# Gated cross-attention and FFN layer: gate values, tanh and Wo^T handled before x(0)^T, u evicted by ScalarE, Z(7) evicted by VectorE

## The chip, the cores and the metric

The kernel runs on one core of a Trainium2 chip. The metric is the device time of one execution in microseconds (us); lower is better. The core has TensorE (PE in the profile, its weight loads PEld), VectorE (DVE), ScalarE (ACT), GpSimd (POOL), and SyncE (SP), which only issues DMA transfers here. Each engine executes its own list of instructions in order; semaphores order the lists against each other.

## The reference

There are 16 batch rows, each of 128 queries and 128 context positions, with 256 features, in float32.

```
LN(x) = (x - mean) / sqrt(var + 1e-5)            over the 256 features
Q = LN(x) @ Wq.T + bq        K = ctx @ Wk.T + bk
attn = softmax(where(mask, -inf, Q @ K.T))
x1 = x + tanh(g_xattn) * ((attn @ ctx) @ Wo.T + bo)
y  = clip(LN(x1) @ sign(W).T * scale + bias, -100, 100)
out = x1 + tanh(g_ffn) * y
```

## The kernel before, in words

All instruction lists are written out by hand; there is no scheduler. The 16 rows are handled as 8 groups of two, numbered 0 to 7; L is 7. The projections of Q and K are folded: the product of Wk and the centred Wq is formed once (wqk), a bias vector u comes with it, and the scores are xn^T times K, where K = wqk applied to ctx^T, plus u. For Z = ctx times Wo^T, Wo^T carries the factor tanh(g_xattn), so the attention output is P times Z directly. Operands of the large products are split in a high and a low fp32r part: ScalarE evicts the high part from PSUM, VectorE subtracts it to get the low part.

For one group TensorE does, in this order: K projection (12 matmuls), transposes of the normalised x of the next group, P times Z of the previous group, scores, transposes of ctx of the next group, transposes of x1 of the previous group, Z projection (12), transposes of the softmax numerators p, and the FFN product of the previous group (8). VectorE computes the residual x1, the masked scores and their minimum (t_sb), the statistics of x1, the low parts x1T_lo and cT_lo, the clip, the FFN scaling (y_scaled), the sum out_sb, and the statistics of x three groups on. GpSimd computes the reciprocal standard deviations (a pow), x + bo (xb_sb, `add_bo`), the mask terms and y_biased. ScalarE evicts K, xT, Z, p^T and the high parts, computes the exponentials and normalises x for groups 2 and up.

The prologue matters for the change. SP issues its transfers in the order Wq, Wk, x(0), ctx(0), Wo, mask, the two gates (4 bytes each), x(1), ctx(1), x(2), bo and so on. TensorE transposes ctx(0), computes u into a few columns of the PSUM bank ps_O, transposes Wo into the bank of Z (L629), waits for the normalised x(0) and transposes it (`transpose_x(0)`), computes the first half of K(0) (L679), broadcasts the two gates over the partitions by a matmul with a row of ones (L818, into other columns of the bank of u; it waits for `u_ready` and for the gates), computes the second half of K(0), transposes ctx(1), and does the scores of group 0 (L721). VectorE evicts u (L557), then xT(0) (L559), then computes the statistics of x(1) (`stats_x(1)`, L427 and L430), then woT_lo (L562). ScalarE evicts the first half of K(0) (L243), computes tanh of both gates (L245), evicts woT_hi with the factor tanh (L248), then the second half of K(0) (L250). GpSimd does the mask terms of group 0, `norm_of_x(1)` (four small operations, L300 to L306), `normalise_x(1)` (L314), `norm_of_x(2)`, then bo times tanh (bo_g, L390), then `add_bo(0)` (L369).

In the tail, TensorE computes the Z of the first row of group 7, the scores of group 7 and the Z of its second row, transposes p (`transpose_p(L)`, L729), does the FFN product of group 6 row by row (`ffn_before_last`), then `attend_last` (L769). VectorE does `mask_and_min(L)` (L455) and then `split_x1T(L - 1)` (L447); `ffn_before_last` waits for the latter. ScalarE does the two exponentials, evicts Z(7) (L219) and then p^T (L230).

Of the kernel before, what the change touches and what calls it, by code (L numbers as in the profile page):

```python
# [6 lines left out]
ACT = mybir.ActivationFunctionType  # L7
# [12 lines left out]
def gated_xattn_ffn(nc, x, ctx, mask, g_xattn, g_ffn, wq, bq, wk, bk, wo, bo, w_ffn, scale_ffn, bias_ffn, out):  # L20
# [12 lines left out]
    G = B // GB  # L33
    T = GB * P
    L = G - 1
# [5 lines left out]
    with ExitStack() as stack:  # L41
# [3 lines left out]
        def sem(name):  # L45
            return stack.enter_context(nc.semaphore(name))

        def bank(name):
# [90 lines left out]
        x1T_hi_done, x1T_lo_done, scaled_done, biased_done, clip_done, out_done, pool_clip_done, pool_out_done = (  # L139
            sem(n) for n in ("x1T_hi_done", "x1T_lo_done", "scaled_done", "biased_done", "clip_done", "out_done",  # L140
                             "pool_clip_done", "pool_out_done"))
        last_biased_done = sem("last_biased_done")

        rows = lambda g: slice(g * GB, (g + 1) * GB)
# [2 lines left out]
        @block.sync  # L147
        def _(sp):
            def load_x(g):
                sp.dma_start(x_sb[:, rows(g), :], x_rows[:, rows(g), :]).then_inc(x_loaded[g], 16)  # L150

            def load_ctx(g):
                sp.dma_start(ctx_sb[:, rows(g), :], ctx_rows[:, rows(g), :]).then_inc(ctx_loaded[g], 16)

            sp.dma_start(wq_sb[:], wq.rearrange("(c p) d -> p c d", p=P)).then_inc(wq_loaded, 16)
            sp.dma_start(wk_sb[:], wk.rearrange("(c p) d -> p c d", p=P)).then_inc(wk_loaded, 16)
            load_x(0)
            load_ctx(0)
            sp.dma_start(wo_sb[:], wo.rearrange("(c p) d -> p c d", p=P)).then_inc(wo_loaded, 16)
            sp.dma_start(mask_u8[:], mask.rearrange("(o b) k -> o b k", o=1).to_broadcast([P, B, P])  # L160
                         ).then_inc(mask_loaded, 16)
            for k, v in enumerate((g_xattn, g_ffn)):
                sp.dma_start(gate_row[:, k:k + 1], v.rearrange("(o d) -> o d", o=1)).then_inc(gates_loaded, 16)
            load_x(1)
            load_ctx(1)
            load_x(2)
            sp.dma_start(bo_sb[:], bo.rearrange("(o d) -> o d", o=1).to_broadcast([P, D])).then_inc(bo_loaded, 16)
            sp.dma_start(w_sb[:], w_ffn.rearrange("(c p) d -> p c d", p=P)).then_inc(w_loaded, 16)
            load_ctx(2)
            load_x(3)  # L170
            sp.dma_start(scale_sb[:], scale_ffn.rearrange("(o d) -> o d", o=1).to_broadcast([P, D])
                         ).then_inc(scale_loaded, 16)
            sp.dma_start(bias_sb[:, 0, :], bias_ffn.rearrange("(o d) -> o d", o=1).to_broadcast([P, D])
                         ).then_inc(bias_loaded, 16)
            load_ctx(3)
            for g in range(4, G):
                load_x(g)
                load_ctx(g)
            for g in range(L):
                if g == L - 2:  # L180
                    sp.wait_ge(pool_out_done, GB)
                else:
                    sp.wait_ge(out_done, g + 1)
                sp.dma_start(out_rows[:, rows(g), :], out_sb[:, rows(g), :]).then_inc(stored, 16)
            for b in range(GB):
                sp.wait_ge(out_done, L + b + 1)
                sp.dma_start(out_rows[:, L * GB + b, :], out_sb[:, L * GB + b, :]).then_inc(stored, 16)
            sp.wait_ge(stored, 16 * (G + 1))

        @block.scalar  # L190
        def _(act):
# [25 lines left out]
            def evict_Z(g):  # L217
                act.wait_ge(Z_prod, g + 1)
                nc.scalar.copy(Z_sb[:, g % 2], ps_Z).then_inc(Z_done, 1)  # L219
# [18 lines left out]
            act.wait_ge(ps_wqk_ready, DC)  # L238
            nc.scalar.copy(wqk_hi[:, 1], ps_wqk[1]).then_inc(wqk_hi_ready, 1)
            evict_cT_hi(0)  # L240
            act.wait_ge(u_ready, 1)
            act.wait_ge(ps_K0_ready, 1)
            nc.scalar.activation(K_sb[:, 0, 0], ps_K0[0], ACT.Identity, bias=u_col[:, 0:1]).then_inc(K_done, 1)  # L243
            act.wait_ge(ps_gates_ready, 1)
            nc.scalar.activation(tanh_g[:], ps_gates, ACT.Tanh).then_inc(tanh_ready, 1)  # L245
            act.wait_ge(ps_woT_ready, 1)
            act.wait_ge(tanh_ready, 1)
            nc.scalar.activation(woT_hi[:], by_chunk(z_bank), ACT.Identity, scale=tanh_g[:, 0:1]).then_inc(woT_hi_ready, 1)  # L248
            act.wait_ge(ps_K0_ready, DC)
            nc.scalar.activation(K_sb[:, 0, 1], ps_K0[1], ACT.Identity, bias=u_col[:, 1:2]).then_inc(K_done, 1)  # L250
            evict_cT_hi(1)
# [26 lines left out]
            evict_x1T_hi(L - 1)  # L278
            exp(L, 0)
            exp(L, 1)  # L280
            evict_Z(L)
            evict_PT(L)

            for b in range(GB):
# [4 lines left out]
        def _(pool):  # L289
# [94 lines left out]
            mask_terms(0)  # L384
            norm_of_x(1)
            normalise_x(1)
            norm_of_x(2)
            pool.wait_ge(tanh_ready, 1)
            pool.wait_ge(bo_loaded, 16)
            nc.gpsimd.tensor_scalar(bo_g[:], bo_sb[:], tanh_g[:, 0:1], 1.0, ALU.mult, ALU.mult).then_inc(bo_g_ready, 1)  # L390
            pool.wait_ge(bo_g_ready, 1)
            add_bo(0)
            mask_terms(1)
# [29 lines left out]
        def _(dve):  # L423
            def stats_x(g):
                dve.wait_ge(x_loaded[g], 16)
                for b in range(GB):
                    nc.vector.bn_stats(bn_x[:, g * GB + b], x_sb[:, g * GB + b]).then_inc(bn_x_done, 1)  # L427
                for b in range(GB):
                    dve.wait_ge(bn_x_done, GB * g + b + 1)
                    nc.vector.bn_aggr(mv_x[:, g * GB + b], bn_x[:, g * GB + b]).then_inc(mv_x_done, 1)  # L430
# [122 lines left out]
            nc.vector.tensor_tensor(wqk_lo[:, 1], ps_wqk[1], wqk_hi[:, 1].bitcast(F32), ALU.subtract  # L553
                                    ).then_inc(wqk_lo_ready, 1)
            split_cT(0)
            dve.wait_ge(ps_u_ready, 1)
            nc.vector.tensor_copy(u_col[:], ps_u).then_inc(u_ready, 1)  # L557
            dve.wait_ge(xT_prod, 1)
            nc.vector.tensor_scalar(xT[:, 0], ps_xT, 1.0, None, ALU.add).then_inc(xT_done, 1)  # L559
            stats_x(1)  # L560
            dve.wait_ge(woT_hi_ready, 1)
            nc.vector.scalar_tensor_tensor(out=woT_lo[:], in0=by_chunk(z_bank), scalar=tanh_g[:, 0:1],  # L562
                                           in1=woT_hi[:].bitcast(F32), op0=ALU.mult, op1=ALU.subtract
# [24 lines left out]
            residual(L - 1)  # L588
            stats_x1(L - 1)
            add_x1(L - 3)  # L590
            mask_and_min(L)
            split_x1T(L - 1)
            for b in range(GB):
                r = L * GB + b
                dve.wait_ge(p_done, r + 1)
# [29 lines left out]
        def _(pe):  # L625
# [136 lines left out]
                accumulate(F_before_last[b], pairs).then_inc(F_prod, 1)  # L762

            def attend_last(b):
                pe.wait_ge(Z_done, G)
                pe.wait_ge(PT_done, GB * L + b + 1)
                if b == 0:
                    pe.wait_ge(x1_done, GB * L)
                nc.tensor.matmul(last_O[b], PT_sb[:, L % 2, b], Z_sb[:, L % 2, b], start=True, stop=True  # L769
                                 ).then_inc(O_prod, 1)  # L770
# [39 lines left out]
            last.then_inc(ps_u_ready, 1)  # L810
            pe.wait_ge(wo_loaded, 16)
            transposes(by_chunk(z_bank), wo_sb).then_inc(ps_woT_ready, 1)
            transpose_x(0)
            project_first_K(0)
            pe.wait_ge(gates_loaded, 32)
            pe.wait_ge(ones_ready, 1)
            pe.wait_ge(u_ready, 1)
            nc.tensor.matmul(ps_gates, ones_row[:], gate_row[:], start=True, stop=True).then_inc(ps_gates_ready, 1)  # L818
            project_first_K(1)
            transpose_ctx(1)  # L820
            first_scores()
# [27 lines left out]
            Z_of(L, 0)  # L849
            scores(L)  # L850
            Z_of(L, 1).then_inc(Z_prod, 1)
            transpose_p(L)
            ffn_before_last(0)
            ffn_before_last(1)
            attend_last(0)
            attend_last(1)
# [31 lines left out]
```

## Time and profile before

| | |
|---|---|
| median of 3 runs | 75.99 us (75.79 to 76.14) |
| profiled execution, its own time | 76.03 us |
| its span in the trace | 74.2 us |
| busy, share of the span: PE / DVE / POOL / ACT | 92% / 78% / 72% / 57% |
| granted TensorE clock | 0.994 of full speed |

All times inside the trace are counted from the start of the span; the execution's own time is 1.8 us longer than the span. Rows of the timeline give the start, the duration, the engine, the line of the kernel, the operation, and the tiles written and read. In brackets stands how long the engine was idle before the row, and which instruction ended the wait.

### The profile page before, as it was taken

The page shows a single profiled execution, that of the slowest core. Times are in us where ns is not written, and L with a number is a line of the kernel's source. Part 1 is how long each engine was busy: PE and PEld are TensorE (multiplying, and loading weights), DVE is VectorE, ACT ScalarE, POOL GpSimd, SP SyncE. Part 2 cuts the span into 40 slices and gives each one's busy share as a digit, 9 for nine tenths or more (in the row PEclk, how much of TensorE's full clock was granted, in tenths as well). Part 3 has the DMA queues.
Part 4 walks back from the last instruction along what each step waited for, and adds up shares of the span by engine and source line. Part 5 has one row for each costly group of instructions (what it writes and reads, how often), then busy time and mean ns, then how long its engine had stood idle before and what let it go on. Part 6 is the DMA issues. An engine that isn't in the chain of part 4 may idle for free.

```text
span 74.2 us, 1595 instructions
## 1 busy us (share of the span) xinstructions
PE 68.2 (92%) x509; PEld 64.1 (86%) x509; DVE 57.8 (78%) x187; ACT 42.4 (57%) x116; POOL 53.7 (72%) x107
## 2 busy tenths in 40 slices
PE   4999999999999999998999999999999999998800
PEld 4988789998999999997999999999999999884500
DVE  0085697894947688699899989998959899759980
ACT  1502519599799639771996397749575906534000
POOL 4000605889899999896989898989899859959700
PEclk9999999999999999999999999999999999999997
DMA  0989999999940000004000400030012000412043
GB/s 4 274 202 335 299 263 309 288 366 357 344 145 5 4 0 9 9 0 141 0 0 0 141 0 9 18 124 0 0 67 75 0 9 0 146 54 87 9 165 109
DMA packets 8229, 8.10 MB, mean 109 GB/s; under 512 B 537, under 2 KB 8093, under 8 KB 8221
## 3 DMA queue, kind: packets, MB, share of 16 engines
q1 hardware_dynamic: 8212, 8.00, 34.7%
q8 instruction: 4, 0.07, 0.4%
q14 instruction: 5, 0.03, 0.2%
q10 hardware_dynamic: 8, 0.00, 0.0%
HBM read 5.90 MB, written 2.10 MB: 108 GB/s over the span
## 4 chain that ended last, share of the span: by engine, by line
PE 45%; POOL 24%; DVE 13%; DMA 6%; issue 4%; ACT 1%; SPq 1%; POOLq 1%; DVEq 0%
PE ps_Z L634 9%; PE ps_K L634 8%; DMA x_sb<-in_x_dram 6%; PE ps_xT L629 6%; PE ps_F L634 6%; POOL xb_sb L369 6%; PE ps_O L737 5%; PE ps_S L634 4%; POOL y_biased L373 4%; POOL rstd_x L302 3%; DVE bn_x L427 3%; PE ps_cT L629 2%; POOL rstd L321 2%; PE ps_S L729 2%; POOL y_clip L346 1%
## 5 line engine op out<-in xcount | busy, mean ns | idle before, releaser
L373 POOL TENSOR_TENSOR y_biased<-y_scaled,bias_g 128x256 f32<-128x256 f32 x14 | 11.7, 857 | 2.1 <-DVE y_scaled L512 1.0
L369 POOL TENSOR_TENSOR xb_sb<-x_sb,bo_g 128x256 f32<-128x256 f32 x16 | 11.4, 736 | 0.1
L224 ACT ACTIVATE p_sb<-t_sb,smin 128x128 f32<-128x128 f32 x16 | 6.4, 401 | 8.1 <-DVE smin L455 8.0
L634 PE MATMUL ps_Z<-woT_hi,cT_hi 128*128 128x256 f32 x32 | 9.8, 305 | 0.0
L214 ACT ACTIVATE K_sb<-ps_K,u_col 128x256 f32<-128x256 f32 x14 | 5.8, 469 | 6.6 <-PE ps_K L634 6.6
L634 PE MATMUL ps_Z<-woT_hi,cT_lo 128*128 128x256 f32 x32 | 9.0, 282 | 0.0
L634 PE MATMUL ps_Z<-woT_lo,cT_hi 128*128 128x256 f32 x32 | 9.0, 282 | 0.0
L466 DVE SCALAR_TENSOR_TENSOR x_sb<-ps_O,recip_p,xb_sb 128x256 f32<-128x256 f32 x14 | 6.1, 479 | 2.9 <-PE ps_O L737 1.8
L634 PE MATMUL ps_K<-cT_hi,wqk_hi 128*128 128x256 f32 x28 | 8.2, 293 | 0.0
L634 PE MATMUL ps_K<-cT_lo,wqk_hi 128*128 128x256 f32 x28 | 7.9, 283 | 0.0
L634 PE MATMUL ps_K<-cT_hi,wqk_lo 128*128 128x256 f32 x28 | 7.9, 283 | 0.0
L634 PEld LDWEIGHTS ps_S<-K_sb,xT 128*128 128x128 f32 x56 | 7.2, 191 | 0.5 <-issue 0.2
L634 PE MATMUL ps_S<-K_sb,xT 128*128 128x128 f32 x56 | 7.5, 277 | 0.0
L737 PE MATMUL ps_O<-Z_sb,PT_sb 128*128 128x256 f32 x28 | 7.2, 379 | 0.0
L634 PE MATMUL ps_F<-wT,x1T_hi 128*128 128x256 f32 x26 | 7.1, 306 | 0.0
L427 DVE BATCH_NORM_STATS2 bn_x<-x_sb 128x6 f32<-128x256 f32 x16 | 5.9, 412 | 1.0 <-DMA x_sb<-in_x_dram 1.0
L442 DVE TENSOR_TENSOR cT_lo<-ps_cT,cT_hi 128x512 fp32r<-128x512 f32 x8 | 5.5, 685 | 1.5 <-ACT cT_hi L197 1.5
L204 ACT ACTIVATE xn<-x_sb,nmr_x,rstd_x 128x256 f32<-128x256 f32 x12 | 6.6, 602 | 0.1
L634 PE MATMUL ps_F<-wT,x1T_lo 128*128 128x256 f32 x26 | 6.5, 282 | 0.0
L512 DVE SCALAR_TENSOR_TENSOR y_scaled<-ps_F,rstd,scale_g 128x256 f32<-128x256 f32 x12 | 5.3, 479 | 1.4 <-POOL rstd L321 1.1
L634 PEld LDWEIGHTS ps_Z<-woT_lo,cT_hi 128*128 128x128 f32 x32 | 6.1, 191 | 0.0
L634 PEld LDWEIGHTS ps_Z<-woT_hi,cT_hi 128*128 128x128 f32 x32 | 6.1, 190 | 0.0
(138 smaller groups left out, 201.9 us busy)
## 6 DMA issues: line engine op xcount, KB each, us to landing
x_sb<-in_x_dram SPq DMA_DIRECT2D x8, 256.0 KB, 7.3
ctx_sb<-in_ctx_dram SPq DMA_DIRECT2D x8, 256.0 KB, 7.2
out_dram<-out_sb SPq DMA_DIRECT2D x7, 256.0 KB, 2.1
wq_sb<-in_L_xattn_Wq_dram SPq DMA_DIRECT2D x1, 256.0 KB, 2.9
wk_sb<-in_L_xattn_Wk_dram SPq DMA_DIRECT2D x1, 256.0 KB, 3.1
wo_sb<-in_L_xattn_Wo_dram SPq DMA_DIRECT2D x1, 256.0 KB, 5.0
mask_u<-in_mask_BxS_bk_dram SPq DMA_DIRECT2D x1, 256.0 KB, 5.4
w_sb<-in_L_ffn_weights_dram SPq DMA_DIRECT2D x1, 256.0 KB, 6.9
```

Of the source, the lines that this page charges most:

```text
L204: nc.scalar.activation(xn[:, r], x_sb[:, r], ACT.Identity, scale=rstd_x[:, r:r + 1], bias=nmr_x[:, r:r + 1]).then_inc(xn_done, 1)
L214: nc.scalar.activation(K_sb[:, g % 2, m], ps_K[:, m], ACT.Identity, bias=u_col[:, m:m + 1]).then_inc(K_done, 1)
L224: nc.scalar.activation(p_sb[:, g % 2, b], t_sb[:, g % 2, b], ACT.Exp, scale=-1.0, bias=smin[:, r:r + 1], accum_out=psum_p[:, r:r + 1]).the ...
L369: nc.gpsimd.tensor_tensor(xb_sb[:, r], x_sb[:, r], bo_g[:], ALU.add).then_inc(xb_done, 1)
L373: nc.gpsimd.tensor_tensor(y_biased[:, g % 2, b], y_scaled[:, g % 2, b], bias_g[:, 0], ALU.add).then_inc(biased_done, 1)
L427: nc.vector.bn_stats(bn_x[:, g * GB + b], x_sb[:, g * GB + b]).then_inc(bn_x_done, 1)
L442: nc.vector.tensor_tensor(cT_lo[:, g % 2], ps_cT, cT_hi[:, g % 2].bitcast(F32), ALU.subtract).then_inc(cT_lo_done, 1)
L466: nc.vector.scalar_tensor_tensor(out=x1_sb[:, r], in0=ps_O[:, b], scalar=recip_p[:, r:r + 1], in1=xb_sb[:, r], op0=ALU.mult, op1=ALU.add). ...
L512: nc.vector.scalar_tensor_tensor(out=y_scaled[:, g % 2, b], in0=ps_F[:, b], scalar=rstd_1[:, r:r + 1], in1=scale_g[:], op0=ALU.mult, op1=A ...
L629: last = nc.tensor.transpose(dst[:, c, b * P:(b + 1) * P], src[:, b, c * P:(c + 1) * P], ident[:])
L634: last = nc.tensor.matmul(dst, lhsT, rhs, start=(n == 0), stop=(n == len(pairs) - 1))
L737: last = nc.tensor.matmul(ps_O[:, b], PT_sb[:, g % 2, b], Z_sb[:, g % 2, b], start=True, stop=True)
```

## The change

SP issues the two gate transfers ahead of the mask. TensorE does the matmul of the gates right after the transposes of Wo, ahead of x(0)^T. The eviction of u goes from VectorE to ScalarE; ScalarE then does tanh and woT_hi ahead of the first half of K(0). VectorE does the statistics of x(1) ahead of the copy of x(0)^T. GpSimd computes bo_g ahead of `norm_of_x(2)`. In the tail VectorE splits x1T(6) before it handles the scores of group 7, and evicts Z(7) after them; TensorE does the first FFN product of group 6 before it transposes p of group 7.

```diff
@@ SP
+            for k, v in enumerate((g_xattn, g_ffn)):
+                sp.dma_start(gate_row[:, k:k + 1], v.rearrange("(o d) -> o d", o=1)).then_inc(gates_loaded, 16)
             sp.dma_start(mask_u8[:], mask.rearrange("(o b) k -> o b k", o=1).to_broadcast([P, B, P])
                          ).then_inc(mask_loaded, 16)
-            for k, v in enumerate((g_xattn, g_ffn)):
-                sp.dma_start(gate_row[:, k:k + 1], v.rearrange("(o d) -> o d", o=1)).then_inc(gates_loaded, 16)
@@ ScalarE
             evict_cT_hi(0)
-            act.wait_ge(u_ready, 1)
-            act.wait_ge(ps_K0_ready, 1)
-            nc.scalar.activation(K_sb[:, 0, 0], ps_K0[0], ACT.Identity, bias=u_col[:, 0:1]).then_inc(K_done, 1)
+            act.wait_ge(ps_u_ready, 1)
+            nc.scalar.copy(u_col[:], ps_u).then_inc(u_ready, 1)
             act.wait_ge(ps_gates_ready, 1)
             nc.scalar.activation(tanh_g[:], ps_gates, ACT.Tanh).then_inc(tanh_ready, 1)
             act.wait_ge(ps_woT_ready, 1)
             act.wait_ge(tanh_ready, 1)
             nc.scalar.activation(woT_hi[:], by_chunk(z_bank), ACT.Identity, scale=tanh_g[:, 0:1]).then_inc(woT_hi_ready, 1)
+            act.wait_ge(u_ready, 1)
+            act.wait_ge(ps_K0_ready, 1)
+            nc.scalar.activation(K_sb[:, 0, 0], ps_K0[0], ACT.Identity, bias=u_col[:, 0:1]).then_inc(K_done, 1)
...
             exp(L, 0)
             exp(L, 1)
-            evict_Z(L)
             evict_PT(L)
@@ GpSimd
             normalise_x(1)
-            norm_of_x(2)
             pool.wait_ge(tanh_ready, 1)
             pool.wait_ge(bo_loaded, 16)
             nc.gpsimd.tensor_scalar(bo_g[:], bo_sb[:], tanh_g[:, 0:1], 1.0, ALU.mult, ALU.mult).then_inc(bo_g_ready, 1)
+            norm_of_x(2)
             pool.wait_ge(bo_g_ready, 1)
@@ VectorE
             split_cT(0)
-            dve.wait_ge(ps_u_ready, 1)
-            nc.vector.tensor_copy(u_col[:], ps_u).then_inc(u_ready, 1)
+            stats_x(1)
             dve.wait_ge(xT_prod, 1)
             nc.vector.tensor_scalar(xT[:, 0], ps_xT, 1.0, None, ALU.add).then_inc(xT_done, 1)
-            stats_x(1)
...
             add_x1(L - 3)
+            split_x1T(L - 1)
             mask_and_min(L)
-            split_x1T(L - 1)
+            dve.wait_ge(Z_prod, G)
+            nc.vector.tensor_copy(Z_sb[:, L % 2], ps_Z).then_inc(last_Z_done, 1)
@@ TensorE
             def attend_last(b):
-                pe.wait_ge(Z_done, G)
+                pe.wait_ge(last_Z_done, 1)
...
             transposes(by_chunk(z_bank), wo_sb).then_inc(ps_woT_ready, 1)
-            transpose_x(0)
-            project_first_K(0)
+
             pe.wait_ge(gates_loaded, 32)
             pe.wait_ge(ones_ready, 1)
             pe.wait_ge(u_ready, 1)
             nc.tensor.matmul(ps_gates, ones_row[:], gate_row[:], start=True, stop=True).then_inc(ps_gates_ready, 1)
+            transpose_x(0)
+            project_first_K(0)
             project_first_K(1)
...
+            ffn_before_last(0)
             transpose_p(L)
-            ffn_before_last(0)
             ffn_before_last(1)
```

## Rows read from the trace of the kernel before

**Rows 1.** Stretches: length; busy us (instructions) of PE, PEld, DVE, ACT, POOL; clock, DMA.
```profile
21.00:34.82 13.82, 13.51 (x110) 13.06 (x108) 10.81 (x33) 9.41 (x26) 12.30 (x24) 1.00 0.09 31
34.82:63.45 28.63, 28.63 (x232) 28.16 (x233) 25.85 (x80) 19.34 (x54) 25.71 (x47) 1.00 0.09 29
```

**Rows 2.** Timeline, TensorE: the gates, K(0), ctx(1) and the first scores.
```profile
9.37 0.42 PEld L629 LDWEIGHTS ps_xT<-ident,xn 128*128 128x128 f32 x4 [0.47 <-DVE xn L550]
...
10.72 0.38 PE L818 MATMUL ps_O<-gate_row,ones_row 1*128 1x2 f32 x2
11.03 0.50 PE L679 MATMUL ps_F<-cT_hi,wqk_hi 128*128 128x256 f32 x2
11.85 0.60 PE L629 MATMUL ps_cT<-ident,ctx_sb 128*128 128x128 f32 x4
...
12.18 0.97 PEld L721 LDWEIGHTS ps_S<-K_sb,xT 128*128 128x128 f32 x8
```

**Rows 3.** Timeline, VectorE at the same place.
```profile
10.16 0.14 DVE L557 COPY u_col<-ps_O 128x2 f32<-128x2 f32 x1
10.23 0.68 DVE L559 TENSOR_SCALAR xT<-ps_xT 128x512 f32<-128x512 f32 x1
10.82 0.74 DVE L427 BATCH_NORM_STATS2 bn_x<-x_sb 128x6 f32<-128x256 f32 x2
11.48 0.30 DVE L430 BATCH_NORM_AGGREGATE mv_x<-bn_x 128x2 f32<-128x6 f32 x2
```

**Rows 4.** DMA issues: size, us to landing; the second from 4.3 to 4.8 us, x(1).
```profile
mask_u<-in_mask_BxS_bk_dram SPq DMA_DIRECT2D x1, 256.0 KB, 5.4
x_sb<-in_x_dram SPq DMA_DIRECT2D x1, 256.0 KB, 5.2
...
3.24 0.47 SPq L160 DMA_DIRECT2D mask_u<-in_mask_BxS_bk_dram  x1
```

**Rows 5.** Timeline, groups 1 and 2: the normalised x and GpSimd.
```profile
13.56 1.10 POOL L314 TENSOR_SCALAR xn<-x_sb,rstd_x,nmr_x 128x256 f32<-128x256 f32 x2
...
15.06 0.71 POOL L302 TENSOR_TENSOR rstd_x<-ve_x,minus_half 128x2 f32<-128x2 f32 x1
...
16.30 0.48 POOL L390 TENSOR_SCALAR bo_g<-bo_sb,tanh_g 128x256 f32<-128x256 f32 x1
...
16.35 1.09 ACT L204 ACTIVATE xn<-x_sb,nmr_x,rstd_x 128x256 f32<-128x256 f32 x2
...
17.68 0.60 PE L629 MATMUL ps_xT<-ident,xn 128*128 128x128 f32 x4
```

**Rows 6.** Waits of TensorE (total, times, longest), then timeline, where it waits and later.
```profile
PEld ps_xT L629 <- DVE x_sb L466: 0.5, 1, 0.5
...
29.95 0.54 DVE L519 TENSOR_SCALAR y_clip<-y_biased,lim 128x512 f32<-128x512 f32 x1
30.06 0.99 POOL L321 TENSOR_TENSOR rstd<-ve,minus_half 128x2 f32<-128x2 f32 x1
31.09 0.88 DVE L512 SCALAR_TENSOR_TENSOR y_scaled<-ps_F,rstd,scale_g 128x256 f32<-128x256 f32 x2 [0.60 <-POOL rstd L321]
...
41.01 0.88 DVE L466 SCALAR_TENSOR_TENSOR x_sb<-ps_O,recip_p,xb_sb 128x256 f32<-128x256 f32 x2
...
41.94 0.43 PEld L629 LDWEIGHTS ps_xT<-ident,x_sb 128*128 128x128 f32 x4
```

**Rows 7.** Timeline of the tail.
```profile
64.16 0.69 DVE L447 TENSOR_TENSOR x1T_lo<-ps_xT,x1T_hi 128x512 fp32r<-128x512 f32 x1
...
64.85 0.14 PEld L729 LDWEIGHTS ps_S<-ident,p_sb 128*128 128x128 f32 x1 [0.25 <-ACT p_sb L224]
...
65.78 0.48 DVE L601 SCALAR_TENSOR_TENSOR y_scaled<-ps_F,rstd,scale_g 128x256 f32<-128x256 f32 x1 [0.78 <-PE ps_F L634]
...
66.34 1.41 POOL L373 TENSOR_TENSOR y_biased<-y_scaled,bias_g 128x256 f32<-128x256 f32 x2 [0.79 <-DVE y_scaled L601]
...
68.93 1.18 POOL L326 TENSOR_TENSOR rstd<-ve,minus_half 128x1 f32<-128x1 f32 x2
```

More of the change, by code:

```diff
@@ L141, in gated_xattn_ffn @@
                              "pool_clip_done", "pool_out_done"))
+        last_Z_done = sem("last_Z_done")
         last_biased_done = sem("last_biased_done")
```

## The prediction

> **What bounds the kernel now.** I read the busy time by stretch first. From 34.82 to 63.45 us TensorE is busy in all 28.63 us, at full clock; from 21.00 to 34.82 it lacks 0.31 us [rows 1]. So the body is TensorE's own work, and a gain must take instructions off TensorE's list or remove one of its few waits. The list of waits names one in the body: the weight load for x1^T waits 0.5 us for VectorE's residual [rows 6]. The timeline then tells why: VectorE had stood idle for 0.60 us before y_scaled at 31.09, until GpSimd's pow had ended [rows 6], and the chain of waits runs back on GpSimd from there, nearly without a gap, to 14.75 us. GpSimd's list from 14.7 to 31 us thus sets TensorE's only stall in the body. The same row of residuals one group later (41.01, 0.88 long, ends 41.89) stands just ahead of the weight load that uses it (41.94) [rows 6]: after the stall VectorE and TensorE run side by side with no reserve, so what TensorE gains at 34.8 is what VectorE gains there, and it is kept to the tail. In the tail the chain is FFN product of group 6, y_scaled (65.78, after 0.78 idle), y_biased on GpSimd (66.34), clip, the last pow (68.93) [rows 7], and then VectorE's last operations and the store.
>
> **The change, part by part.**
>
> *Gates ahead of x(0)^T.* The matmul of the gates starts at 10.72 and the second half of K(0) at 11.03, so it takes 0.31 us of TensorE's path [rows 2]. Its new place is a gap: PEld is idle for 0.47 us before 9.37, that is from 8.90 on, waiting for the normalised x(0) [rows 2]. Before its wait it has to see u evicted: the u matmuls end at about 8.65, and a copy of 128x2 takes 0.14 on VectorE [rows 3]; on ScalarE the row is not there for this shape, and I take 0.2 (tanh of the same shape is the nearest; bounds 0.14 and the 0.3 that would put it at 8.95). The matmul can then start at 8.95 and is through by 9.27, 0.1 ahead of need. If the cover is gone, it costs what it overlaps, at most 0.31, and the gain of this step is nothing. Then also the gates must have landed. No row gives their landing. They now take the mask's place in the list, issued at 3.24 and some 0.4 later; the mask issued there landed 5.4 later, at 8.64 [rows 4]. I take that as the bound from above for the first and 8.7 for the second, still ahead of 8.95. From below it is somewhere after their issue, which costs nothing. The mask itself is issued 0.6 later and lands at about 9.3; its term on GpSimd (0.4 us) falls in an idle stretch that lasts until the statistics of x(1), so nothing is late.
>
> The Trainium skill (DMA: Bandwidth & Descriptors, Queues, rings and completion order) says that completion is not FIFO per issuing engine, and that a one-engine copy can complete while earlier 16-engine ones are still open. Its table of the fixed cost gives about 2.0 us; an estimate by it has the gates in by 5.7 to 8.7 us, on the same side as the bound above. No row shows their landing.
>
> *K(0), xT(0), statistics.* The second half of K(0) now follows the first directly and takes 0.82 us as before (11.03 to 11.85) [rows 2]. The weight load for the scores, at 12.18 before, could be at 11.8. What may be late instead is xT(0), now behind the statistics: VectorE drops the u copy and starts the statistics at 10.16 instead of 10.82 (0.66 earlier), and the copy of xT ends where the statistics ended, 11.78 [rows 3], less 0.07 for the u copy: 11.7. That is just in time. x(1) landed at about 9.6 (issued near 4.4, 5.2 to landing) [rows 4], 0.5 before it is needed. ScalarE has tanh and woT_hi (0.7 us) behind it at about 10.4, before the first half of K(0) is ready at 10.8, and evicts both halves without being late. So the scores move by 0.3 to 0.4.
>
> *Normalised x(1), bo_g, normalised x(2).* Statistics 0.66 earlier put GpSimd's xn(1) at 12.90 instead of 13.56, ending 14.00 [rows 5]; TensorE wants it at about 14.4. Then bo_g (0.48) runs to 14.5, in what would else be a wait for the statistics of x(2). bo landed at about 12.5. The pow of x(2) moves from 15.06 by 0.2 only, and ScalarE's xn(2), 16.35 to 17.44, moves to 17.24 at the end. Its transposes stood at 17.68 [rows 5] and can be at 17.34 at the earliest. This caps TensorE's gain in the prologue at about 0.3. I take 0.3 (bounds 0, if the gates' cover fails, and 0.4). But `add_bo(0)`, the next on GpSimd, gains both: 0.2, and 0.48 because bo_g no longer stands before it: 0.67.
>
> *The stall at 34.8.* GpSimd's list runs from there to the pow at 30.06 without waiting, as far as I can follow its inputs: y_scaled of group 0 is ready at about 24.1 and wanted at 24.6, the statistics of x(4) at 24.9 and wanted at 26.0, those of x1(1) at 28.1 and wanted at 29.1. So the pow ends 0.67 earlier and y_scaled starts at 30.42 instead of 31.09. VectorE is free for it at 30.2 (the clip ends at 30.49 [rows 6], less 0.3). So the residual that TensorE waits for is 0.67 earlier. TensorE without the stall would be earlier by 0.3 of the prologue plus 0.31 (its idle) to 0.5 (that of the weight load), 0.6 to 0.8. The smaller of both is 0.62 to 0.67; I take 0.65 for prologue and stall together. Bounds: 0.3 if nothing of the stall goes, 0.8 if all of it does.
>
> The pow took 0.99 there and 0.71 for the same shape at 15.06 [rows 5, 6], while VectorE's clip ran beside it. The Trainium skill (SBUF — State Buffer, Who interferes with whom) has a cause: VectorE and GpSimd share a port pair, and an operation in a two-port mode blocks the other for its whole length. By that rule a pow that starts 0.67 earlier and a clip that starts 0.3 earlier still overlap, by about 0.2 instead of 0.4, and the residual could gain up to 0.2 more than I take. In other places the same rule can make new collisions, the subject of the last rival.
>
> *Tail.* VectorE's split of x1T(6) (0.69, the next operation starts 0.61 after it) goes ahead of the scores. Its input is there at 63.14, so it ends at 63.8 and the first t_sb starts 0.19 later than before (63.78 instead of 63.59). The second one waited for its scores and is late by 0.06 only. Both exponentials are late by 0.19, and the transpose of the second p, which PEld did at 64.85 after 0.25 idle [rows 7], could be at 65.05. TensorE fills this with the first FFN product (4 matmuls, 0.49), which starts at 64.47 and ends at 64.96; the two transposes then find p ready at once. The second FFN product ends 0.25 to 0.3 earlier. Z(7) is evicted by VectorE at 64.65 (its last matmul ends at 64.60); the price is that of the xT copy of the same shape, 0.68 [rows 3], so to 65.33, with `attend_last` wanting it at 65.6. It falls in VectorE's 0.78 idle before y_scaled [rows 7]; behind it stand the two reciprocals (0.23) and y_scaled, which starts at 65.5 instead of 65.78. So y_biased, the clips and the last pow start 0.27 earlier; the variance that the pow also needs moves with the residuals, 0.27. I take 0.27. Bounds: minus 0.2 (VectorE's three additions to the wait all come late) and plus 0.35.
>
> *Sum.* 0.65 + 0.27 = 0.92; 76.03 - 0.92 = 75.11 us against the profiled execution. That one is 0.04 above the median of the runs shown, so 75.1 stands.
>
> **Rivals.**
>
> *A. Only TensorE's own 0.3 comes, the stall stays.* GpSimd's chain is caught by an input, or bo_g waits for tanh or bo, so that y_scaled at 31.09 moves only with TensorE. For it: the stage has several inputs with under 1 us of reserve. Against: the reserves worked out above. 76.03 - 0.3 - 0.27 = 75.46, between 75.3 and 75.6.
>
> *B. The change does not do what it says at the front.* The gates land late (they are only known to have been there at 10.72 [rows 2]) or xT(0) takes the place of K(0) as what the scores wait for. TensorE's list is in order, so all stands behind the gates. With a landing at 9.4 the 0.3 is gone; at 10.2, half a microsecond ahead of when they were used, x(0)^T starts 1.1 late, of which the direct K(0) halves and the stall give back most. Remaining: the tail. 76.03 - 0.27 = 75.76, up to 76.0.
>
> *C. Slower: VectorE and GpSimd collide in the body.* From 34.82 on the two lists have no reserve to TensorE [rows 6]. GpSimd's place relative to VectorE shifts by about 0.3 (0.67 against 0.3) at least up to the stall. A collision like that of the pow, 0.99 instead of 0.71, is 0.28. If one more of them falls in each of the four full groups from 34.8 on and VectorE's list pays it, that is 1.1, and with the 0.92 taken off 76.03 - 0.92 + 1.1 = 76.2; if it starts already in groups 1 and 2, 1.7 and 76.8. It decides from the point where VectorE's loop per group is over TensorE's by more than 0.23 (0.92 shared by four). Against: from 34.8 on GpSimd itself waits for VectorE's statistics once per group or follows directly, so that their places relative to each other are restored.
>
> *D. Better than forecast:* the second half of K(0) 0.1 cheaper, and the pow without collision: 74.7.
>
> **How the numbers follow.** Forecast 0.58 (own range 74.85 to 75.3), A 0.19, B 0.11, C 0.07, D 0.05. A range of 74.8 to 75.75 holds the forecast, A, and the near end of B, and leaves out C, most of D and the far end of B: about 0.17. About 0.5% (0.38 us) can be told from no change here, so faster is below 75.61: the forecast, A nearly whole and D, 0.82; same is B and a little of A and C, 0.12; slower, above 76.37, 0.06 with the far part of C.
>
> **What would show it.** The matmul of the gates before 9.3, x(0)^T still at 9.4: step one right. The scores' weight load at 11.8 to 11.9 and xn(2)'s transposes at about 17.35: prologue right, with its cap. `add_bo(0)` at 16.2 instead of 16.87 and y_scaled of group 1 at about 30.4: the second step. No wait of TensorE for x_sb near 34: the stall is gone. In the tail, Z(7)'s copy between 64 and 65.4 less the shift, and y_scaled with less idle before it. A wait of TensorE for the gates, a longer period than 7.12 us per group, or the stall unchanged would make it wrong.

## The result, and the profile after

The changed kernel takes 74.88 us (median of 4 runs, 74.61 to 75.35) against 76.06 us of the kernel before (4 runs), a ratio of 0.987 (95% interval 0.983 to 0.991). Twelve more runs of it beside 35 of the kernel before gave 75.18 against 75.93, ratio 0.992 (0.988 to 0.995). The two intervals overlap; the larger set says 0.75 us, the smaller 1.18, the forecast was 0.92. The profiled execution took 75.10 us, span 73.3. The ratios compare fast executions alone (left out is, for instance, one of 88.88 us with a granted clock of 0.768), so that a ratio is not the quotient of the two medians beside it.

The stretches of the changed kernel, columns as in [rows 1], with one more for the prologue:

```profile
9.37:14.00 4.63, 4.63 (x41) 4.45 (x40) 3.33 (x12) 2.79 (x8) 2.91 (x7) 1.00 1.03 276
...
21.00:34.82 13.82, 13.82 (x115) 13.56 (x114) 11.35 (x37) 9.75 (x28) 12.22 (x24) 1.00 0.11 37
34.82:63.45 28.63, 28.63 (x234) 28.12 (x233) 26.35 (x78) 19.01 (x54) 25.90 (x45) 1.00 0.08 29
```

TensorE now has no idle from 21.00 to 34.82 us either: the 0.31 us of [rows 1] is gone, and its list of waits holds none for x_sb before the tail. The timeline of the prologue of the changed kernel, the answer to [rows 2, 3, 5]:

```profile
9.58 0.29 PEld L819 LDWEIGHTS ps_O<-gate_row,ones_row 1*128 1x128 f32 x2 [0.17 <-issue]
9.63 0.74 DVE L429 BATCH_NORM_STATS2 bn_x<-x_sb 128x6 f32<-128x256 f32 x2
...
9.89 0.42 PEld L631 LDWEIGHTS ps_xT<-ident,xn 128*128 128x128 f32 x4
...
12.15 0.97 PEld L723 LDWEIGHTS ps_S<-K_sb,xT 128*128 128x128 f32 x8
...
13.46 0.48 POOL L391 TENSOR_SCALAR bo_g<-bo_sb,tanh_g 128x256 f32<-128x256 f32 x1
...
14.71 0.22 POOL L302 TENSOR_SCALAR ve_x<-mv_x 128x2 f32<-128x2 f32 x1 [0.78 <-DVE mv_x L432]
...
16.25 1.43 POOL L371 TENSOR_TENSOR xb_sb<-x_sb,bo_g 128x256 f32<-128x256 f32 x2
```

The scores' weight load starts at 12.15, hardly before the 12.18 of [rows 2]. Yet add_bo(0) starts at 16.25 instead of 16.87. These are its rows in the kernel before, with GpSimd's first operation on x(1), and the weight load that waits in the middle:

```profile
11.87 0.23 POOL L300 TENSOR_SCALAR ve_x<-mv_x 128x2 f32<-128x2 f32 x1 [2.70 <-DVE mv_x L430]
...
16.87 1.41 POOL L369 TENSOR_TENSOR xb_sb<-x_sb,bo_g 128x256 f32<-128x256 f32 x2
...
34.82 0.42 PEld L629 LDWEIGHTS ps_xT<-ident,x_sb 128*128 128x128 f32 x4 [0.55 <-DVE x_sb L466]
```

The rest of the changed kernel, first GpSimd's operation on x(1) and the transposes of x(2), then the answer to [rows 6]:

```profile
10.68 0.23 POOL L302 TENSOR_SCALAR ve_x<-mv_x 128x2 f32<-128x2 f32 x1 [1.74 <-DVE mv_x L432]
...
17.65 0.60 PE L631 MATMUL ps_xT<-ident,xn 128*128 128x128 f32 x4
...
29.50 0.99 POOL L323 TENSOR_TENSOR rstd<-ve,minus_half 128x2 f32<-128x2 f32 x1
...
30.53 0.88 DVE L514 SCALAR_TENSOR_TENSOR y_scaled<-ps_F,rstd,scale_g 128x256 f32<-128x256 f32 x2
...
34.31 0.62 PE L631 MATMUL ps_xT<-ident,x_sb 128*128 128x128 f32 x4
```

y_scaled of group 1 is 0.56 us earlier, with no idle before it that the row would show, and the transposes of x1 follow without a wait. The transposes of x(2) are only 0.03 us earlier than in [rows 5], but the first matmul of K(4) is 0.55 us earlier (37.39 for 37.94): in this profile nearly all of TensorE's gain ahead of the tail is the stall. The tail, the answer to [rows 7]:

```profile
62.68 0.69 DVE L449 TENSOR_TENSOR x1T_lo<-ps_xT,x1T_hi 128x512 fp32r<-128x512 f32 x1
...
64.16 0.69 DVE L594 COPY Z_sb<-ps_Z 128x512 f32<-128x512 f32 x1 [0.37 <-PE ps_Z L636]
...
64.76 0.21 DVE L598 RECIPROCAL recip_p<-psum_p 128x1 f32<-128x1 f32 x2
...
64.89 0.47 DVE L603 SCALAR_TENSOR_TENSOR y_scaled<-ps_F,rstd,scale_g 128x256 f32<-128x256 f32 x1
...
65.44 1.41 POOL L375 TENSOR_TENSOR y_biased<-y_scaled,bias_g 128x256 f32<-128x256 f32 x2 [0.43 <-DVE y_scaled L603]
```

GpSimd waits 0.43 us for y_scaled where it waited 0.79. The scores of group 7 and VectorE's last operation, in the kernel before and in the changed one:

```profile
62.77 1.12 PE L634 MATMUL ps_S<-K_sb,xT 128*128 128x128 f32 x8
...
71.64 0.42 DVE L503 TENSOR_TENSOR out_sb<-y_clip,x_sb 128x256 f32<-128x256 f32 x1
```

```profile
62.28 1.12 PE L636 MATMUL ps_S<-K_sb,xT 128*128 128x128 f32 x8
...
70.74 0.43 DVE L505 TENSOR_TENSOR out_sb<-y_clip,x_sb 128x256 f32<-128x256 f32 x1
```

### The profile page after: what moved, and what is told of

It reads as the page before. It is cut to its first block, busy times and chain, and to the rows that moved or that the text cites. A ratio compares the mean times of both kernels' runs of the same rounds, so it can differ in the third digit from the quotient of the medians.

```text
span 73.3 us, 1595 instructions
## 1 busy us (share of the span) xinstructions
PE 68.0 (93%) x509; PEld 64.5 (88%) x509; DVE 59.0 (80%) x187; ACT 42.6 (58%) x116; POOL 53.8 (73%) x107
## 4 chain that ended last, share of the span: by engine, by line
PE 86%; DVE 5%; POOL 3%; POOLq 1%; issue 1%
PE ps_Z L636 16%; PE ps_K L636 14%; PE ps_S L636 12%; PE ps_xT L631 9%; PE ps_O L739 8%; PE ps_F L636 8%; PE ps_F L791 6%; PE ps_cT L631 5%; PE ps_S L731 2%; POOL y_biased L375 2%; POOL y_clip L348 1%; DVE y_biased L494 1%; PE ps_S L723 1%; PE ps_O L636 1%; DVE out_sb L505 1%; PE ps_F L681 1%
## 5 line engine op out<-in xcount | busy, mean ns | idle before, releaser
L636 PEld LDWEIGHTS ps_Z<-woT_hi,cT_lo 128*128 128x128 f32 x32 | 6.1, 190 | 0.0
```

What stands on the lines that cost most here:

```text
L636: last = nc.tensor.matmul(dst, lhsT, rhs, start=(n == 0), stop=(n == len(pairs) - 1))
```

## The experiments

Times are medians; "before" is the kernel before, run on the same chip in between. The first four kernels of the table shared one set of runs of the kernel before, the next four another, the last four a third.

| kernel | us | before | ratio (95%) |
|---|---|---|---|
| changed kernel again | 75.18 | 75.93 | 0.992 (0.988 to 0.995) |
| front only | 75.59 | 75.93 | 0.995 (0.991 to 0.998) |
| tail only | 75.62 | 75.93 | 0.995 (0.991 to 0.998) |
| bo_g only | 76.05 | 75.93 | 1.002 (0.998 to 1.005) |
| bo_g back | 75.48 | 75.86 | 0.992 (0.988 to 0.996) |
| statistics of x(1) back | 75.69 | 75.86 | 1.000 (0.997 to 1.004) |
| gates behind the mask | 75.10 | 75.86 | 0.991 (0.987 to 0.994) |
| Z(7) by ScalarE | 75.09 | 75.86 | 0.992 (0.988 to 0.996) |
| mask behind ctx(1) | 75.35 | 75.98 | 0.991 (0.988 to 0.995) |
| and statistics of x(2) early | 75.59 | 75.98 | 0.992 (0.988 to 0.995) |
| same, bo_g first | 75.37 | 75.98 | 0.990 (0.987 to 0.994) |
| and affine on VectorE | 75.24 | 75.98 | 0.991 (0.988 to 0.994) |

**The changed kernel again.** No edit.

> The changed kernel itself, profiled once more. In its first profile the weight loads between 5.1 and 6.4 us took 0.33 us each instead of 0.19, so that ctx(0) was transposed 0.5 us later than in the kernel before. If that stretch belongs to the single execution and not to the change, another profile can show ctx(0) transposed at about 7.3 and a span of about 72.8 us, and the median stays between 74.6 and 75.1. If the change itself causes it (fewer or other transfers early), it comes back in this profile with a span of 73.3 us or more.

The late start is of the execution, not of the change: ctx(0) was transposed at 7.77 us in the first profile and at 7.35 in this one, and with the old prologue it was at 7.26 to 8.10. But a different thing came in its place, in the timeline of this second profile:

```profile
10.88 0.75 DVE L429 BATCH_NORM_STATS2 bn_x<-x_sb 128x6 f32<-128x256 f32 x2 [1.17 <-DMA x_sb<-in_x_dram]
...
12.48 0.97 PEld L723 LDWEIGHTS ps_S<-K_sb,xT 128*128 128x128 f32 x8 [0.41 <-DVE xT L560]
...
18.16 0.42 PEld L631 LDWEIGHTS ps_xT<-ident,xn 128*128 128x128 f32 x4 [0.42 <-ACT xn L205]
```

x(1) landed 1.2 us after VectorE wanted it. Everything behind the statistics waits, the copy of xT(0) too, and TensorE waits 0.41 us for that and 0.42 us for the normalised x(2). The span is 73.9 us, 0.6 more than in the first profile.

**Front and tail apart.** In the first the tail is that of the kernel before, in the second all else is.

> All of the change except the tail. My theory: prologue and stall give their 0.65 us, and up to 1.0 if the gain of the start goes through whole, so 75.0 to 75.4; no wait of TensorE for x_sb near 34 us. Rival (the gain is nearly all tail): 75.8 to 76.0.

> The tail of the change alone on the kernel before. My theory: 0.27 (by the prediction) to 0.41 us (by the two traces, from the start of the Z matmuls of the second row of group 7 to the end of the last VectorE operation: 8.42 before, 8.01 after), so 75.65 to 75.8; the stall at 34 us stays. Rival (prologue and tail need each other, since TensorE's early arrival made the room): no change, 75.9 to 76.1.

0.34 us by the front, 0.31 us by the tail; together 0.65, about the 0.75 of the whole. They add, as far as intervals of 0.1 to 0.7 us for each part can tell. From the start of the scores of group 7 to the start of the last VectorE operation the six profiles of the table's first four rows and of both original kernels give 8.87 us with the old tail (three) and 8.45 or 8.46 with the new one (three): 0.41 to 0.42 us for the tail, whatever stands before it.

**bo_g alone, and bo_g back.** The two edits are each other's inverse, on the kernel before and on the changed one:

```diff
+            nc.gpsimd.tensor_scalar(bo_g[:], bo_sb[:], tanh_g[:, 0:1], 1.0, ALU.mult, ALU.mult).then_inc(bo_g_ready, 1)
             norm_of_x(2)
-            nc.gpsimd.tensor_scalar(bo_g[:], bo_sb[:], tanh_g[:, 0:1], 1.0, ALU.mult, ALU.mult).then_inc(bo_g_ready, 1)
```

> On the kernel before, only bo_g goes ahead of norm_of_x(2). My theory: add_bo(0) and all of GpSimd's list behind it start 0.48 us earlier, y_scaled of group 1 starts 0.48 earlier (30.6 instead of 31.09), and the wait of 0.3 to 0.5 us of TensorE for x_sb near 34 us goes, so 75.55 to 75.75. Cost if bo_g delays the normalised x(2): its transposes 0.1 to 0.4 us late. Rival (the stall goes because TensorE and VectorE start earlier, not because of GpSimd's list): the stall stays and the time is 75.9 to 76.1.

> The changed kernel with bo_g back behind norm_of_x(2). My theory: the transposes of x(2) need not wait for GpSimd any more (K(1) to the transposes of x(2) 2.39 us instead of 2.57 in the second profile of the changed kernel), but add_bo(0) is late by 0.3 to 0.5 and TensorE's wait for x_sb near 34 us is back with 0.3 to 0.5 us, so 0.1 to 0.4 us slower than the changed kernel. Rival, after bo_g alone on the kernel before brought nothing: moving bo_g is worth nothing here either, since what goes at 34 us is paid at 18 us; same time within 0.1.

The rival of the second won. Of the first, my theory had the wait right, which is gone near 34 us, and the rival had the time: TensorE waits as long for the normalised x(2) instead, and no time is gained. From its timeline:

```profile
14.52 0.48 POOL L389 TENSOR_SCALAR bo_g<-bo_sb,tanh_g 128x256 f32<-128x256 f32 x1
...
16.90 1.41 POOL L369 TENSOR_TENSOR xb_sb<-x_sb,bo_g 128x256 f32<-128x256 f32 x2
...
18.11 0.42 PEld L629 LDWEIGHTS ps_xT<-ident,xn 128*128 128x128 f32 x4 [0.69 <-ACT xn L204]
...
34.95 0.61 PE L629 MATMUL ps_xT<-ident,x_sb 128*128 128x128 f32 x4
```

add_bo(0) starts at 16.90, as before at 16.87: GpSimd had nothing to wait for between the normalised x(1) and x(2), so exchanging two parts of its list moves nothing behind both. With bo_g back in the changed kernel the wait near 34 us is back, here from the timeline of that kernel:

```profile
14.78 0.22 POOL L302 TENSOR_SCALAR ve_x<-mv_x 128x2 f32<-128x2 f32 x1 [0.95 <-DVE mv_x L432]
...
34.87 0.66 PE L631 MATMUL ps_xT<-ident,x_sb 128*128 128x128 f32 x4 [0.32 <-DVE x_sb L468]
```

and the ratio is the same, 0.992. The pair of profiles differs all the same: GpSimd began with x(2) at 14.71 and at 14.78 us, after waiting 0.78 and 0.95 us for its statistics, and add_bo(0) followed at 16.25 with bo_g ahead and at 16.90 with it behind. Where there is such a gap, bo_g does fit into it; no gain from it shows in the times of the runs.

**Statistics of x(1) back.**

```diff
             split_cT(0)
-            stats_x(1)
             dve.wait_ge(xT_prod, 1)
             nc.vector.tensor_scalar(xT[:, 0], ps_xT, 1.0, None, ALU.add).then_inc(xT_done, 1)
+            stats_x(1)
```

> The changed kernel with the xT(0) copy ahead of the statistics of x(1) again. My theory: with x(1) late (10.85 us in the second profile) the scores no longer wait for xT(0) and start at 12.1 instead of 12.48, but the statistics, the normalised x(1) and x(2) come 0.3 to 0.6 later and TensorE waits at the transposes of x(2): same time or up to 0.3 us slower. Rival: the order with the statistics first costs more than it brings, because x(1) often lands late; then this one is 0.1 to 0.4 us faster.

By the ratio nothing is left of the gain, and the three kernels measured beside it have 0.991 or 0.992, with intervals that end at 0.996 at most, below the 0.997 where this one's begins. So the place of the statistics counts, and my 0.3 us was too small. How all of it can go is not shown: the new tail is still in this kernel and takes 8.46 us in its profile, as in the changed one, so that its 0.3 to 0.4 us should be left; the medians leave 0.17. Its profile had an early start, the scores of group 0 at 11.76 us, the earliest of all fourteen profiles, and TensorE then lost the lead again, 0.4 us of weight load waiting for GpSimd's normalised x(1) and 0.7 for ScalarE's x(2). Its waits:

```profile
ACT xn L205 <- POOL nmr_x L308: 0.9, 1, 0.9
...
PEld ps_xT L631 <- ACT xn L205: 0.7, 1, 0.7
...
PEld ps_xT L631 <- POOL xn L316: 0.4, 1, 0.4
```

**What sets the body.** I put the starts from the timelines side by side: GpSimd's first operation on the statistics of x(1), its start of add_bo(0), and the first matmul of K(4) on TensorE.

| kernel | x(1) on GpSimd | add_bo(0) | K(4) | add_bo(0) to K(4) |
|---|---|---|---|---|
| before | 11.87 | 16.87 | 37.94 | 21.07 |
| changed | 10.68 | 16.25 | 37.39 | 21.14 |
| changed again | 11.94 | 16.95 | 38.06 | 21.11 |
| front only | 11.70 | 16.72 | 37.84 | 21.12 |
| tail only | 12.11 | 17.20 | 38.27 | 21.07 |
| bo_g only | 11.75 | 16.90 | 38.02 | 21.12 |
| bo_g back | 11.03 | 16.90 | 37.99 | 21.09 |
| statistics back | 11.74 | 16.65 | 37.77 | 21.12 |
| gates behind mask | 11.28 | 16.29 | 37.41 | 21.12 |
| Z(7) by ScalarE | 11.39 | 16.41 | 37.52 | 21.11 |

The last column is constant within 0.07 us, while TensorE's own start of the scores of group 0 varies from 11.76 to 12.62. The column before it follows the first one by 4.9 to 5.15 us, unless GpSimd has to wait for the statistics of x(2) (0.78 and 0.95 us, in the changed kernel and with bo_g back). So I took GpSimd's list from the statistics of x(1) on as what sets where TensorE stands at 38 us. The last four kernels of the table of times were made on this reading.

For the kernels with bo_g ahead the waits confirm this only up to x(2). There the transposes of x(2) start 1.21 or 1.22 us after add_bo(0), and K(4) 19.90 or 19.91 us after those (1.40 and 19.74 in the first profile of the changed kernel, where TensorE had no wait for x(2)), and TensorE is never idle from 21.00 to 34.82: that part is TensorE's own list. With bo_g behind, TensorE has no wait for x(2), and K(4) comes 20.24 to 20.27 us after its transposes, the wait for x_sb included; there it is GpSimd's list up to the pow. The same 21.1 us is made of different parts in the two orders.

**Gates behind the mask.** SP's order of before, all else changed.

> The changed kernel with the two gate transfers behind the mask again, as before the change. My theory: the gates land well before TensorE gets to their matmul (9.2 to 9.6 us), also 0.6 us later; no wait for them in the profile, and the same time within 0.15 us. Rival: the gates land with the mask (about 9.1 to 9.4 us here); TensorE then waits 0.2 to 0.6 us for them and the kernel is slower by that.

No profile of any kernel with the gates first has a wait for the gates; TensorE's row for them says 0.17 us of issue in all of them. With the mask ahead of them the matmul ran at 9.22, with the same 0.17. Moving their transfers brought nothing that these runs can tell.

**Z(7) by ScalarE.** `evict_Z(L)` back between exponentials and p^T, the order of the rest of the tail kept.

> The changed kernel with Z(7) evicted by ScalarE between the exponentials and p^T again; the order of the split and of the first FFN product stays changed. My theory: ScalarE's Z copy (0.56) stands before p^T, so attend_last starts 0.1 to 0.3 later, but VectorE is free for y_scaled 0.6 earlier: y_scaled then follows the first FFN product (about 64.6 in place of 64.9) and GpSimd's y_biased, the head of the last chain, moves earlier by up to 0.3. The last pow needs the variance of x1(7) too, so what comes last is attend_last: 0 to 0.2 us slower than the changed kernel. Rival (the eviction by VectorE makes the gain of the tail): 0.3 to 0.4 slower. Second rival (the order alone makes it): same.

Same time; the tail by the measure above takes 8.53 us, 0.07 more. The gain of the tail is the order (split and FFN product first; the two were not tried apart), not the engine that evicts.

**Mask behind ctx(1); statistics of x(2) early.**

```diff
             load_x(1)
             load_ctx(1)
+            sp.dma_start(mask_u8[:], ...).then_inc(mask_loaded, 16)
             load_x(2)
@@ VectorE, in the second and third kernel
+            stats_x(2)
             mask_and_min(0)
-            stats_x(2)
```

> The changed kernel with the mask transfer issued behind x(1) and ctx(1). In all ten profiles so far the K projection of group 4 starts 21.07 to 21.14 us after GpSimd starts add_bo(0), and add_bo(0) starts 4.9 to 5.15 us after GpSimd's first operation on the statistics of x(1), unless GpSimd has to wait for those of x(2). My theory: GpSimd's list sets the body; x(1) issued 0.6 us earlier lands earlier, VectorE waits 0.3 to 0.6 us less for it, GpSimd starts on it at 10.7 to 11.0 instead of 11.3 to 11.9, and the K projection of group 4 starts at 37.1 to 37.4 instead of 37.4 to 38.1: 0.1 to 0.4 us faster than the changed kernel, about 74.8. Rival (x(1) lands when its bytes have come, whatever the order, or the mask is late now): same or slower by up to 0.3.

> As mask_behind, and VectorE computes the statistics of x(2) ahead of the masked scores of group 0, where it waits up to 1.3 us for TensorE, and bo_g is behind norm_of_x(2) again. My theory: GpSimd no longer waits for the statistics of x(2) (0.8 to 0.95 us in two profiles), so add_bo(0) starts 5.0 us after its first operation on x(1), about 15.9, x(2) is normalised 0.5 us ahead of add_bo(0) and its transposes wait for nothing, the wait near 34 us stays or is what GpSimd's list makes of it; K projection of group 4 at about 37.0: 0.3 to 0.7 us faster than the changed kernel, 74.4 to 74.8. Rival (x(2) lands after 11.9 us): VectorE stands at it and the scores of group 0 are late: slower.

> As stats2_early but with bo_g ahead of norm_of_x(2). My theory: GpSimd's list is without a gap in either order, so add_bo(0) starts at the same time and the K projection of group 4 too; only the place of TensorE's wait differs (transposes of x(2) here, x_sb near 34 us there): same as stats2_early within 0.15 us. Rival (the order of bo_g matters by itself): they differ by 0.3 us or more.

None of the three is faster than the changed kernel: 0.990 to 0.992, as it. x(1) was early now, and the rival was right for a reason that I had overlooked in GpSimd's list. From the timeline of the kernel with the mask behind ctx(1):

```profile
9.50 0.74 DVE L429 BATCH_NORM_STATS2 bn_x<-x_sb 128x6 f32<-128x256 f32 x2
...
11.56 0.41 POOL L365 TENSOR_SCALAR mask_add<-mask_u 128x256 f32<-128x256 uint8 x1 [3.73 <-DMA mask_u<-in_mask_BxS_bk_dram]
...
12.05 0.23 POOL L302 TENSOR_SCALAR ve_x<-mv_x 128x2 f32<-128x2 f32 x1
...
16.96 0.73 POOL L371 TENSOR_TENSOR xb_sb<-x_sb,bo_g 128x256 f32<-128x256 f32 x1
...
38.07 0.28 PE L636 MATMUL ps_K<-cT_hi,wqk_hi 128*128 128x256 f32 x1
```

The mask terms of group 0 stand ahead of x(1) in GpSimd's list, the mask landed at 11.5, and GpSimd began with x(1) at 12.05 though its statistics had ended 1.6 us earlier. The rest follows as the table of starts says: add_bo(0) 4.9 later, K(4) 21.1 after that. In the second and third kernel the first operation on x(1) is at 12.02 and 11.58, for the same cause. With bo_g first K(4) comes 21.13 us after add_bo(0), with it last 20.79, and the times do not differ by what can be told. The 20.79 against 21.07 to 21.09 of the other kernels with bo_g last fits the pow near 30 us, which took 0.71 us here and 0.97 to 0.99 there. A version with the mask terms behind x(1) in GpSimd's list was not tried.

**Affine terms on VectorE.** On top of the second of these.

```diff
             stats_x(3)
+            nc.vector.tensor_scalar(scale_g[:], scale_sb[:], tanh_g[:, 1:2], 1.0, ALU.mult, ALU.mult)
+            nc.vector.tensor_scalar(bias_g[:, 0], bias_sb[:, 0], tanh_g[:, 1:2], 1.0, ALU.mult, ALU.mult)
```

> As stats2_early, and VectorE computes scale_g and bias_g (2 x 128x256) behind the statistics of x(3), where it waited 0.75 to 1.0 us for add_bo(0); GpSimd's list is shorter by 0.96 us before the reciprocal deviations of x1(0). My theory: if GpSimd's list from add_bo(0) to the pow near 30 us sets the body, TensorE's wait for x_sb near 34 us (0.3 to 0.6 us) goes and the kernel is 0.3 to 0.5 us faster than stats2_early, about 74.2. Rival (VectorE's list is as long and now pays): x1(0) is late by 0.5, no gain over stats2_early or slower.

TensorE's wait near 34 us is gone, and K(4) starts 20.57 us after add_bo(0) instead of 20.79: of 0.96 us less on GpSimd only 0.2 arrive, since TensorE's own work from the transposes of x(2) (17.69) to K(4) (37.39) takes 19.70. The ratio is that of the others, and the 0.3 to 0.5 us that I expected did not come.

## Why the prediction was right

The time (75.1 forecast, 74.88 and 75.18 measured) came as forecast, and both halves brought a gain. That the sum is so near is in part luck: the front term, 0.65, was too large and the tail term, 0.27, too small, and the steps behind them are uneven.

*Gates ahead of x(0)^T, 0.3 to 0.4 us.* Right only in some executions. The wait in which the gates were to hide, 0.47 us of weight load in [rows 2], is there if x(0) lands late against the wqk products. The row of those 8 matmuls has 1.96 us in the profile that I read, and 1.89 to 2.69 in the others. From the transposes of ctx(0) to the scores the kernel before took 5.03 us; but "tail only" and "bo_g only", with the same prologue list at this place and no wait for x(0), took 4.52 and 4.51, and the kernels with the gates first 4.48 to 4.58 (5.13 where x(1) was late). Where there is no wait, moving the gates is worth nothing. The 2.0 us that the prediction takes from the Trainium skill (DMA: Bandwidth & Descriptors, Anatomy of one DMA — SWDGE (gpsimd) path) stands there for transfers that GpSimd issues, and these are SyncE's. No row shows when the gates land, only that their matmul ran without a wait for them at 9.08 us in the earliest case.

*Normalised x(1), bo_g, x(2).* The statistics of x(1) did move GpSimd (first operation at 10.68 for 11.87), and taken back they cost 0.6 to 0.7 us by the ratios, against the kernels measured beside it, more than the front alone brought; so they carry the front, though the sizes do not add up. The cap by the normalised x(2) was real and is the wait of TensorE in the front-only, the gates and the Z(7) kernels (0.4 us each) and the second profile. The sentence that add_bo(0) gains 0.48 us because bo_g no longer stands before it is right only in some executions. In the kernel before, GpSimd has no gap for bo_g to fill; the gap of 0.55 us that I filled comes only if its list reaches x(2) before the statistics do, and of the profiles of kernels with bo_g ahead only the first has more of it than bo_g takes. My own number for add_bo(0), 16.2, was met (16.25) there by luck: x(1) was on GpSimd at 10.68, 0.5 us earlier than I had worked out, and 0.78 us of waiting was left.

*The stall.* It disappears as forecast, and its cause, GpSimd's list, is what the runs show: with 0.96 us taken off that list the wait is gone with bo_g behind as well. But it is one of two places where TensorE waits for the same list; which one depends on the order of bo_g. The size of the step was not as worked out: VectorE's clip started at 29.92 and not 0.3 earlier than 29.95, as TensorE was not ahead in this profile (K(3) at 30.24 for 30.28), so y_scaled (30.53 for my 30.42) was held up by VectorE itself.

*0.65 us for both.* Measured 0.34 by the front alone (interval 0.1 to 0.7). The term was mis-sized. It took x(1) as landed 0.5 us ahead of need, by one profile; in the second profile of the changed kernel VectorE waited 1.17 us for it and in the front-only one 0.57, and K(4) stood 0.12 us later and 0.10 earlier than in the kernel before. It also counted the gates' 0.3 us in full. How much of the difference each makes is not shown.

*Tail, 0.27 us.* Measured 0.41 to 0.42 in the traces, 0.31 by the clock of the runs (interval 0.2 to 0.7). The mechanism is as described; I had added full durations. Behind the Z copy (0.69) the reciprocals start 0.60 later and y_scaled 0.13 after these, 0.73 instead of my 0.91.

*Rivals.* A did not come as such, though its condition (an input catches GpSimd's chain) did in part. B is half true: the gates were never late, but xT(0) was, in the second profile. C did not come: from K(4) to K(5) and from K(5) to K(6) it is 7.14 and 7.16 us (7.12 and 7.14 in the kernel before), and 7.12 to 7.15 in the others. The pow at 29.50 still took 0.99 us beside the clip, so the gain that the rule on the shared port pair in the Trainium skill (SBUF — State Buffer, Who interferes with whom) left open did not arise. The rows bear that rule out only in part: by it the later of two such operations is blocked until the first has ended, but here the pow is the earlier one and is the one lengthened, and elsewhere neither is. Two groups later in the changed kernel a pow of 0.71 us had the whole clip beside it, and in the kernel with the statistics of x(2) early a clip that had started 0.08 us before the pow did not lengthen it. First the two pairs of the changed kernel, then that one:

```profile
29.50 0.99 POOL L323 TENSOR_TENSOR rstd<-ve,minus_half 128x2 f32<-128x2 f32 x1
29.92 0.54 DVE L521 TENSOR_SCALAR y_clip<-y_biased,lim 128x512 f32<-128x512 f32 x1
...
44.11 0.71 POOL L323 TENSOR_TENSOR rstd<-ve,minus_half 128x2 f32<-128x2 f32 x1
44.20 0.54 DVE L521 TENSOR_SCALAR y_clip<-y_biased,lim 128x512 f32<-128x512 f32 x1
```

```profile
30.14 0.55 DVE L521 TENSOR_SCALAR y_clip<-y_biased,lim 128x512 f32<-128x512 f32 x1
30.22 0.71 POOL L323 TENSOR_TENSOR rstd<-ve,minus_half 128x2 f32<-128x2 f32 x1
```

So a clip beside it is not enough to lengthen the pow; the moment at which the clip starts counts, as told in the last section. No row says whether this clip runs in a two-port mode, and the cause stays open.

## What to carry to other kernels

A wait in one profile that is to hide work has to be traced to what ends it: if that is a transfer, another execution may not have it, and a move into it is worth nothing there. Look for the distance between two events that stays constant over many profiles; it says where to look, but follow the waits inside it before it is put down to one engine: here a constant 21.1 us was GpSimd's list in one order and mostly TensorE's own in the other. Before a transfer or an operation is moved ahead, read what stands behind its neighbour in every in-order list: exchanging two parts of a list without a gap moves nothing, and a transfer made late holds up all that its first user's engine does next.

## What the runs showed of the hardware

The same transfer was there at very different times in different executions of kernels with the same transfers ahead of it: VectorE's first operation on x(0) came at 5.13 us without a wait in one profile and, after waiting, at 6.68 in another. The first matmuls of one execution can be slower while the granted clock is given as 1.00, full speed: the weight loads of wqk between 5.1 and 6.4 us took 0.33 us each in the first profile of the changed kernel and about 0.19 in that of the kernel before. Runs of one kernel on one chip spread by 1.1 us (75.37 to 76.50 for the kernel before), so that of steps of 0.3 us only the traces tell. What a clip on VectorE (128x512, 0.54 us) does to a pow on GpSimd (128x2, 0.71 us alone) goes by the moment at which it starts. Over all profiles the pow took 0.97 to 0.99 us when the clip had started 0.11 to 0.13 us before it or started 0.42 after it, 0.93 to 0.95 when it started 0.35 to 0.38 after it, and 0.71 when it started 0.08 before it, 0.09 to 0.13 after it or 0.44 to 0.49 after it; the clip kept its 0.54 or 0.55. On VectorE two equal operations side by side, scale_g and bias_g of 128x256, took 0.34 and 0.89 us in the last kernel, the second beside GpSimd's add_bo(0).
